# A fused layer-norm, gated mixer and int8 product: another sign for the centred rows, a shorter quantisation step, and the first norm's shift on GpSimd

## The reference

```python
h = einsum('bhid,oi,od->bho', x, weighted_sum, weight)     # image rows
h = concatenate([h, txt], axis=1)                          # 589 rows of 256
n = layernorm(h)                                           # (h - mean) / sqrt(var + 1e-5)
gate = sigmoid(relu(n @ w1 + b1) @ w2 + b2)
glob = gate * (n @ U) * cumsum(n @ V, axis=rows)
h = h + conv3(n) + glob @ out_w + out_b
n = layernorm(h)
s = max(abs(n), axis=-1) / 127                             # one step for each row
acc = round(n / s) @ round(rhs / rs)                       # integers; rs: a step for each column
out = h + acc * s * rs
```

## Time and profile before

| | |
|---|---|
| median of 3 runs | 128.95 us (128.38 to 129.08) |
| the profiled execution | 129.47 us |
| its span, first to last instruction | 127.7 us |
| PE busy | 109.4 us (86%) |
| DVE busy | 88.2 us (69%), 266 instructions |
| ACT busy | 59.3 us (46%), 128 instructions |
| POOL busy | 49.5 us (39%), 91 instructions |
| mean granted TensorE clock | 0.967 of full speed |

### The profile page before, as it was taken

The page is one execution under the profiler, slowest core; times in us unless marked ns, Lnnn a source line. Parts: engine busy times, 40 slices in busy tenths (PEclk is TensorE's granted clock), DMA queues, the critical chain, the costliest instruction groups (busy, mean ns, idle before and its releaser), DMA issues.

```text
span 127.7 us, 1866 instructions
## 1 busy us (share of the span) xinstructions
PE 109.4 (86%) x568; PEld 88.3 (69%) x568; DVE 88.2 (69%) x266; ACT 59.3 (46%) x128; POOL 49.5 (39%) x91
## 2 busy tenths in 40 slices
PE   6169999999999999999979999998995389199960
PEld 6057886687886988788658868866882277099740
DVE  0251440659519688975978898599689999978962
ACT  4000037564632584747247582934485846315520
POOL 2000042002202437171637646360947437416840
PEclk9999999999999999999999999999999959968997
DMA  2999999992000000000022000002020001300014
GB/s 86 253 362 285 397 417 424 424 421 85 0 0 0 0 0 0 8 0 0 0 82 81 1 27 5 0 0 85 0 82 25 0 0 41 124 5 25 0 41 148
DMA packets 5447, 12.55 MB, mean 98 GB/s; under 512 B 471, under 2 KB 3391, under 8 KB 4671
## 3 DMA queue, kind: packets, MB, share of 16 engines
q1 hardware_dynamic: 5151, 11.93, 25.9%
q10 hardware_dynamic: 288, 0.52, 1.4%
HBM read 10.04 MB, written 2.41 MB: 98 GB/s over the span
## 4 chain that ended last, share of the span: by engine, by line
PE 58%; DVE 21%; DMA 8%; issue 3%; ACT 3%; SPq 2%; POOL 2%; DVEq 0%; POOLq 0%
PE h_ps L708 31%; DMA txt_sb<-txt_dram 8%; DVE convT L603 6%; DVE csum L591 5%; PE uvg_ps L766 5%; PE h_ps L790 4%; PE xt_ps L824 3%; PE qt_ps L806 3%; DVE stats L542 3%; DVE tmp L669 3%; PE acc_ps L817 2%; PE h_ps L793 2%; SPq L299 2%; PE xt_ps L752 2%; PE uvg_ps L773 2%
## 5 line engine op out<-in xcount | busy, mean ns | idle before, releaser
L708 PE MATMUL h_ps<-w_tok,x_sb 128*128 128x256 f32 x256 | 64.6, 396 | 3.9 <-DVE w_tok L537 3.9
L708 PEld LDWEIGHTS h_ps<-w_tok,x_sb 128*128 128x128 f32 x256 | 48.3, 198 | 13.1 <-DMA x_sb<-x_dram 4.2
L542 DVE BATCH_NORM_STATS2 stats<-h_ps 128x6 f32<-128x256 f32 (+1 forms) x36 | 13.9, 422 | 12.0 <-PE h_ps L793 6.6
L340 POOL TENSOR_SCALAR rstd<-mv 128x2 f32<-128x2 f32 (+2 forms) x21 | 4.7, 226 | 40.5 <-DVE mv L545 40.0
L378 POOL TENSOR_SCALAR v<-xc,qmul 128x256 f32<-128x256 f32 (+1 forms) x20 | 10.7, 540 | 16.6 <-DVE qmul L647 16.4
L603 DVE SCALAR_TENSOR_TENSOR convT<-xnT,par_sb,convT 128x255 f32<-128x255 f32 (+1 forms) x32 | 16.4, 567 | 0.0
L341 POOL TENSOR_TENSOR rstd<-rstd,exponent 128x2 f32<-128x2 f32 (+2 forms) x21 | 14.9, 711 | 1.7
L494 ACT ACTIVATE xc<-h_ps,nmean 128x256 f32<-128x256 f32 (+1 forms) x20 | 8.6, 469 | 10.7 <-DVE nmean L619 10.7
L470 ACT ACTIVATE glob<-glob 32x256 fp32r<-32x256 f32 (+1 forms) x16 | 7.2, 448 | 11.9 <-POOL glob L352 6.3
L484 ACT ACTIVATE xn<-h_ps,shift,rstd 128x256 f32<-128x256 f32 x16 | 8.2, 563 | 8.7 <-DVE shift L631 8.6
L352 POOL TENSOR_TENSOR glob<-gate,us 32x256 f32<-32x256 f32 x8 | 6.6, 830 | 13.6 <-ACT gate L461 13.6
(11 more groups left out here) (75 smaller groups left out, 141.0 us busy)
## 6 DMA issues: line engine op xcount, KB each, us to landing
x_sb<-x_dram SPq DMA_DIRECT2D x6, 1024.0 KB, 17.2
out_dram<-fin SPq DMA_DIRECT2D x8, 256.0 KB
x_sb<-x_dram SPq DMA_DIRECT2D x4, 256.0 KB, 6.5
x_sb<-x_dram SPq DMA_DIRECT2D x2, 512.0 KB, 9.8
wt_sb<-wt_dram ACTq DMA_DIRECT2D x2, 256.0 KB, 4.7
txt_sb<-txt_dram SPq DMA_DIRECT2D x1, 308.0 KB
out_dram<-fin SPq DMA_DIRECT2D x4, 77.0 KB
par_sb<-par_dram SPq DMA_DIRECT2D x1, 277.0 KB, 10.6
```

The source lines that it names most:

```text
L542: last = nc.vector.bn_stats(stats[0:rows, t, :], src(t))
L708: last = nc.tensor.matmul(h_of(g)[:, t, :], x_sb[:, g, kc, t * P:(t + 1) * P], w_tok[:, kc, :], start=(kc == 0 and t == 0), stop=(kc == KC ...
```

## The change

Three things are changed. The centred rows have the other sign: ACT writes `xc` = mean - h straight from `mv2` with a scale of -1, so that `nmean2` and its instruction are gone. The quantisation step is made from the largest value alone: `nstep` = -max(amax, floor)/127 in one instruction, and `qmul` is its reciprocal. The step times `rstd2`, which the output's scale wants, is made later, ahead of `tmp` in the stage `out`. The sign of `rs_row` is turned as well, so that the signs cancel. And `shift1` is made on POOL, directly behind `rstd1`, with one instruction for each column of the group (two) or for each batch of the text rows (four).

```diff
-                nc.vector.tensor_scalar(rs_row[:, :], acc_ps[:, 0:D], 1.0 / INT8_MAX, None,
+                nc.vector.tensor_scalar(rs_row[:, :], acc_ps[:, 0:D], -1.0, None,
...
+            def shift(out_ap, mean_ap, rstd_ap, done):
+                for t in range(out_ap.shape[1]):
+                    last = nc.gpsimd.tensor_scalar(out_ap[:, t:t + 1], mean_ap[:, t:t + 1], -1.0,
+                                                   rstd_ap[:, t:t + 1], ALU.mult, ALU.mult)
+                last.then_inc(done, 1)
...
+                    pool.wait_ge(txt_rstd, 1)
+                    shift(shift1[0:T, 2 * GROUPS:2 * GROUPS + B], mv1[0:T, 2 * GROUPS:2 * GROUPS + B, 0],
+                          rstd1[0:T, 2 * GROUPS:2 * GROUPS + B], txt_shift)
...
                     rsqrt(rstd1[:, 2 * g:2 * g + 2], mv1[:, 2 * g:2 * g + 2, 1], rstd1_ready)
+                    pool.wait_ge(rstd1_ready, g + 1)
+                    shift(shift1[:, 2 * g:2 * g + 2], mv1[:, 2 * g:2 * g + 2, 0], rstd1[:, 2 * g:2 * g + 2],
+                          shift1_ready)
...
-                    act.wait_ge(nmean2_ready, j + 1)
+                    act.wait_ge(var2_ready, j + 1)
...
-                                                    ACT.Identity, bias=nmean2[0:rows, j, t:t + 1])
+                                                    ACT.Identity, scale=-1.0, bias=mv2[0:rows, j, t, 0:1])
...
-                    dve.wait_ge(var2_ready, j + 1)
-                    nc.vector.tensor_scalar(nmean2[0:rows, j, 0:nt], mv2[0:rows, j, 0:nt, 0], -1.0, None,
-                                            ALU.mult).then_inc(nmean2_ready, 1)
...
-                for g in groups(tick, "shift"):
-                    dve.wait_ge(rstd1_ready, g + 1)
-                    nc.vector.scalar_tensor_tensor(out=shift1[:, 2 * g:2 * g + 2],
-                                                   in0=mv1[:, 2 * g:2 * g + 2, 0], scalar=-1.0,
-                                                   in1=rstd1[:, 2 * g:2 * g + 2], op0=ALU.mult,
-                                                   op1=ALU.mult).then_inc(shift1_ready, 1)
...
-                    dve.wait_ge(rstd2_ready, j + 1)
-                    for t in range(nt):
-                        last = nc.vector.tensor_scalar(ls[:, t:t + 1], a[:, t:t + 1], rs[:, t:t + 1], SCALE_FLOOR,
-                                                       ALU.mult, ALU.max)
-                    then_wait(last)
-                    then_wait(nc.vector.reciprocal(a, ls))
-                    nc.vector.scalar_tensor_tensor(out=qm, in0=a, scalar=INT8_MAX, in1=rs, op0=ALU.mult,
-                                                   op1=ALU.mult).then_inc(qmul_ready, 1)
+                    then_wait(nc.vector.tensor_scalar(am, a, SCALE_FLOOR * LN_EPS ** 0.5, -1.0 / INT8_MAX,
+                                                      ALU.max, ALU.mult))
+                    nc.vector.reciprocal(qm, am).then_inc(qmul_ready, 1)
...
                 for j in items(tick, "out"):
                     _, _, nt, rows = item(j)
+                    dve.wait_ge(rstd2_ready, j + 1)
+                    then_wait(nc.vector.tensor_tensor(lscale[0:rows, j, 0:nt], nstep[0:rows, j, 0:nt],
+                                                      rstd2[0:rows, j, 0:nt], ALU.mult))
                     dve.wait_ge(acc_done, j + 1)
```

More of the change, by code:

```diff
@@ L23 @@
 PARTS = 4
-GROUP_AT = dict(stats=0, rstd=0, shift=1, norm=2, turn=3, move=6, hidden=7, relu=8, sums=8, gates=9,
+GROUP_AT = dict(stats=0, rstd=0, norm=2, turn=3, move=6, hidden=7, relu=8, sums=8, gates=9,
                 sigmoid=11, gated=10, high=12, low=13, mid=7, tap0=9, tap2=10)
@@ L31 @@
                fin=13)
-GROUP_AT_LAST = dict(stats=0, rstd=0, shift=0, norm=1, turn=4, move=4, hidden=5, relu=8, sums=6,
+GROUP_AT_LAST = dict(stats=0, rstd=0, norm=1, turn=4, move=4, hidden=5, relu=8, sums=6,
                      gates=9, sigmoid=11, gated=11, high=11, low=12, mid=8, tap0=10, tap2=11)
@@ L40 @@
 FIN_ON_DVE = 10
-TXT_AT = dict(stats=0, rstd=4, shift=4, norm=7, turn=10, move=9, hidden=11, relu=11, uv=9, gates=12,
+TXT_AT = dict(stats=0, rstd=4, norm=7, turn=10, move=9, hidden=11, relu=11, uv=9, gates=12,
               sigmoid=14)
@@ L157, in early_fusion_kernel @@
         rstd2 = sb("rstd2", [P, ITEMS, 2])
-        nmean2 = sb("nmean2", [P, ITEMS, 2])
         amax = sb("amax", [P, ITEMS, 2])
+        nstep = sb("nstep", [P, ITEMS, 2])
         lscale = sb("lscale", [P, ITEMS, 2])
@@ L279, in early_fusion_kernel @@
         rstd2_ready = sem("rstd2_ready")
-        nmean2_ready = sem("nmean2_ready")
         xc_ready = sem("xc_ready")
@@ L552, in txt_stats @@
                 statistics(stats1[:, TX:TX + B, :], mv1[:, TX:TX + B, :], lambda b: txt_sb[:, b, :], B, T, txt_var)
[L554 to L558, removed]
             def rhs_round():
@@ L628, in _ @@
                                             glob3[0:R, b % 2, lo:hi].bitcast(F32), ALU.subtract).then_inc(glob_low, 1)
-                for g in groups(tick, "shift"):
-                    dve.wait_ge(rstd1_ready, g + 1)
-                    nc.vector.scalar_tensor_tensor(out=shift1[:, 2 * g:2 * g + 2],
-                                                   in0=mv1[:, 2 * g:2 * g + 2, 0], scalar=-1.0,
-                                                   in1=rstd1[:, 2 * g:2 * g + 2], op0=ALU.mult,
-                                                   op1=ALU.mult).then_inc(shift1_ready, 1)
                 for j in items(tick, "scale"):
                     _, _, nt, rows = item(j)
-                    a, ls, qm, rs = (z[0:rows, j, 0:nt] for z in (amax, lscale, qmul, rstd2))
+                    a, am, qm = (z[0:rows, j, 0:nt] for z in (amax, nstep, qmul))
                     dve.wait_ge(xc_ready, j + 1)
@@ L685, in _ @@
                     txt_stats()
-                if tick == TXT_AT["shift"]:
-                    txt_shifts()
                 if tick == TXT_AT["uv"]:
```

## The result

The changed kernel takes 132.19 us (median of 4, 130.96 to 132.51), the kernel before in the same comparison 128.66: ratio 1.027, 95% interval 1.022 to 1.032. It is 3.5 us slower. Times are medians of all runs of a kernel; ratios and intervals leave out runs that lay over 1.5% above the fastest of the same kernel. The profiled execution took 132.01 us with a span of 130.2, 2.54 us more than before.

The account below looks back on a forecast made before the run. Bound: TensorE's chain, with waits for the text norm, for DVE's taps and in batch 3 for v. Terms 0.73 + 1.0 + 1.0 - 0.4 + 0.2 = +2.5: 132.0 us profiled, 131.5 as a median, range 128.6 to 133.2.

Parts of the forecast that it names:

- Text shift: At the text rows: four small POOL instructions delay ACT's xn_txt and so the idle TensorE, +0.73 us (bounds +0.13 to +1.1).
- Second halves of batches 1 and 2: Later fin and the lscale product delay tmp and the taps, so TensorE waits +1.0 us in each (bounds +0.13 to +1.64).
- signs that I had named for these batches: Batches 1 and 2: text csum over 1 us, lscale over 0.5, TensorE's wait for the taps 1 us longer in each.
- passing rival: Batches 1 and 2: csum goes ahead of POOL's pair, lscale ahead of glob; each half costs 0.13; 129.75 us, chance 0.23.
- overtaking rival: Batches 1 and 2: fin overtakes the taps as in batch 3, +1.64 us per half; 132.8 us, chance 0.26.
- The rule weighed there: Second halves: the first of POOL's two small instructions shuts out the text csum, fin then follows, giving the +1.0 us.
- First half of batch 3: Earlier norm and qmul let v finish sooner, held only by glob behind the taps: -0.4 us (bounds 0 to -1.05).
- the bound of -1.05: First half of batch 3: the gain if glob gets in ahead of the taps, -1.05 us.
- End: Last product for the output's scale stands between the last but one fin and tmp: +0.2 us (0 to 0.25).
- a clock that might not fall: Batch 3: glob ahead of the taps shortens TensorE's stop, its clock may stay full, saving 1.5 us; 127.0 us, chance 0.13.
- groups 1 to 3 at nothing: Groups' shifts with idle engines: POOL's pair replaces 0.3 us and TensorE turns these rows a microsecond later, so no cost.

Follow-up runs that it names:

- e3: The changed kernel with only the text rows' shift back on DVE, the groups' shift still on POOL: 131.10 us, ratio 1.018.
- e1: The changed kernel with both shifts, text and groups, back on DVE: 128.82 us, no ratio given.
- e7: The changed kernel with both shifts back on DVE and the product nstep * rstd2 made behind the reciprocal: 127.36 us, ratio 0.990.
- e8: The changed kernel with POOL writing zeros instead of the last addition (fin) of items 0 and 3: 134.10 us in one execution.
- e6: The kernel before with the shorter quantisation step alone, its product ahead of tmp: 128.34 us, ratio 0.998.
- e9: The changed kernel with POOL writing zeros instead of the last addition (fin) of items 0, 1, 3 and 4: 130.33 us in one execution.
- e11: The changed kernel with fin of items 0 and 3 due one tick earlier, ahead of rstd and shift: 133.65 us, ratio 1.042.
- e2: The kernel before with only the shifts moved to POOL: 132.83 us, ratio 1.033.
- e4: The changed kernel with the product nstep * rstd2 made behind the reciprocal instead of ahead of tmp: 131.39 us, ratio 1.021.
- e5: The kernel before with the centring alone (nmean2 gone, sign turned in rs_row): 127.89 us, ratio 0.992.
- e10: e7 with fin of items 0 and 3 due one tick earlier, ahead of rstd: 126.07 us, ratio 0.983.

## Why the prediction was right

The time (131.5 said, 132.19 measured, range 128.6 to 133.2) and the direction were right. By terms:

- *Text shift*: +0.73 said, +0.90 measured (e3: 0.92). Right in kind; an instruction took 0.25 from start to start, not 0.2, and the wait on POOL's own result 0.11. The 0.52 us of idle TensorE that I took from the earlier trace rows is the weight load's; its matmuls had been idle for 0.14. So there was less of a wait than I thought, and where the text lands earlier it is gone (e1, e7): the term is paid in full only in some executions.
- *Second halves of batches 1 and 2*: +1.0 said for each, +1.42 and +1.41 measured. The place, the cause and the 0.2 of the product were right, and the bounds (0.13 to 1.64) held. The step that failed is the one in the middle: "I take it that the text `csum` waits for it as it did". It did not; `us_txt` did. Nor was the product held: it was issued 0.13 ahead of `glob`. And I had the taps run free in 1.99, where the second `fin` cost them a microsecond. Two of the signs that I had named for these batches, `csum` over 1 us and `lscale` over 0.5, are absent. What happened is what the passing rival said of `csum` and `lscale`, without its gain, and then most of the overtaking one, with one tap getting through ahead of `fin`. I had laid out both and gave the forecast to a path between them that did not occur; 1.42 lies nearer to the overtaking rival's 1.64 than to my 1.0.
- The rule weighed there, that a POOL instruction issued first shuts DVE out for its length ("SBUF — State Buffer", section "Who interferes with whom", of the Trainium skill), fits `fin` and the wide `glob` wherever a DVE instruction with two SBUF inputs came behind them in the halves. For the pair of small ones it would have given `csum` a wait, and `csum` took 0.39 though issued 0.04 behind the first. Nor did it hold to the end of `glob`'s text part (65.30 to 65.64): the tap issued at 65.48 took its usual 0.55. The same section's sentence that a DVE instruction with two SBUF inputs contends only with a GpSimd instruction that reads SBUF is borne out by e8: `us_txt` 0.23 beside a POOL instruction that only writes.
- *First half of batch 3*: -0.4 said, -0.72 measured. `glob` was not held by the taps but got in between them, part of what I had as the bound of -1.05.
- *End*: +0.2 said for the product. The trace shows it (`lscale` at 126.86 behind `fin`). Of the traces with a second stretch at the lower clock, those with the product ahead of `tmp` end in 13.52 to 13.53 (e6, e8, e9, e11) and those without in 13.26 to 13.29 (e2, e4, e5, e7, e10); the kernel before, 13.55 without it, does not fit, and why is open. In the changed kernel it lies under a clock that moved: +0.55 and -0.83 in the last two segments. I had foreseen a clock that might not fall, not one that falls once for longer and is then full for the end.
- *Not foreseen*: +0.27 in batch 0. Every kernel with the groups' shift on POOL has it (40.68 to 40.69 for 40.4; e9 and e11 with the clock's loss on top), and the taps there took 2.47 for 1.99: `glob` comes 0.3 sooner against them and gets in ahead of the last one, which takes 1.03 for 0.56. I had priced groups 1 to 3 at nothing, looking only at when TensorE needs the norm.

The sum was nearer than its parts, because shortfalls in batches 0 to 2 and in the text (1.3 together) were partly balanced by batch 3 and the end (0.8 less than said; 0.2 of it goes with the clock, since e9 and e11, the same there but for two stretches at 0.50, take 19.85 for the last two segments and the changed kernel 19.65). That is luck. The overtaking rival's 132.8 is no farther from the measured 132.19 than the 131.5 of the forecast.

## What to carry to other kernels

Before moving a small instruction from DVE to GpSimd, list what stands behind it in GpSimd's queue and lay it on DVE's timeline: 0.5 us of small work cost 1.2 us each time (e1) and in the old kernel 1.6 (e2), by what it pushed and by what it released sooner, not by itself. Taking away one of two collisions gave back next to nothing (0.14 to 0.18; e8, e11) and both gave back everything (e9), so a single undoing that shows no gain does not clear its suspect. When a span starts with a DMA that lands at another time in each run, compare stretches between events.

## What the runs showed of the hardware

- GpSimd instructions on 77x1 or 128x1 came 0.25 us apart, the first behind a wait on its own engine's result 0.1 us later; the same shift on DVE took 0.16 in one instruction.
- DVE's text sum and `us_txt` (two SBUF inputs, 32x77) took 0.39 and 0.23 us beside these small GpSimd instructions (changed kernel, e11), and `us_txt` 0.23 beside one of 0.53 that only writes (e8), but 1.36 beside an addition of 128x512.
- Who gets in between is not settled. A tap issued 0.16 us before the end of `glob`'s text part passed ahead of `fin`, and the next took 1.57. A tap issued while `glob` itself ran waited in most cases for it, its text part and `fin` in one piece (1.9 to 2.6 us: e4, e8, e11, and batch 3 of the kernel before). But in e9, issued in the same place as in e8, it got in between `glob` and the text part (1.03 for 2.56 us), and so did one in batch 3 of e2, with an addition to follow (0.61).
- Waits of 1.2 us (changed kernel) and 1.7 (e2) on TensorE ahead of the text transposes left its clock full, waits of 2.0 (e9) and 2.6 (e11) at the same place were followed by 0.50 and cost 1.4 us. The length of a stop alone does not settle it: in batch 3, stops of 1.50 and 1.78 us were followed by 0.50 in the changed kernel, and stops of 1.50 and 1.85 at the same place left the clock full in e4.
